# Layer 1's q projection computed transposed, for two tiles at a time

## The reference

```
x = x + tanh(g_xattn[0]) * L0_xattn(layernorm(x), ctx)   # 32 heads of 128, 8 key/value heads, rms-normed q and k
x = x + tanh(g_ffn[0])   * L0_ffn(layernorm(x))          # routed LoRA: 8 experts of rank 16
x = x + tanh(g_xattn[1]) * L1_xattn(layernorm(x), ctx)   # 16 heads of 96, 4 key/value heads, q and k not normed
x = x + tanh(g_ffn[1])   * L1_ffn(layernorm(x))          # silu(gate) * up, then down
```

```
q = (latents @ Wq.T).reshape(b, q_len, H, HD)            # H = 16, HD = 96
q = q.transpose(0, 2, 1, 3).reshape(b, KV, G, q_len, HD) # KV = 4 groups of G = 4 heads
scores = einsum('bkgqd,bksd->bkgqs', q, k) * scale       # contracted over the 96 of a head
```

## Time and profile before

| | us |
|---|---|
| median of 3 runs | 1289.04 |
| lowest and highest run | 1287.67, 1289.56 |
| the profiled execution: its own time | 1291.96 |
| the profiled execution: span from first to last instruction | 1290.1 |

### The profile page before, as it was taken

How to read it: one execution, slowest core, us unless ns; L and a number is a source line. 1 busy time by engine, 2 the same in 40 slices (tenths; PEclk the granted TensorE clock), 3 DMA queues, 4 the chain that set the end, 5 groups by cost and what they waited for, 6 DMA issues and landing times.

```text
span 1290.1 us, 24439 instructions
## 1 busy us (share of the span) xinstructions
PE 1254.1 (97%) x7392; PEld 1103.9 (86%) x7392; DVE 962.0 (75%) x2425; ACT 830.8 (64%) x2867; POOL 582.9 (45%) x1029
## 2 busy tenths in 40 slices
PE   8799999999999999999999989999999999999998
PEld 7698888888888888888888878899999999878886
DVE  7778777867787787787778888887777778963434
ACT  6677777767777777787778655576666666632221
POOL 3566555556565565566555642332333323540000
PEclk9899999999999999999999999999999999999999
DMA  6465465554455654544655431333543324370000
GB/s 211 92 131 115 83 135 105 113 110 103 102 115 103 130 106 95 123 109 86 134 113 101 102 71 34 69 72 70 103 91 66 85 57 101 73 179 1 33 1 33
DMA packets 339078, 121.11 MB, mean 94 GB/s; under 512 B 307104, under 2 KB 325280, under 8 KB 338976
## 3 DMA queue, kind: packets, MB, share of 16 engines
q1 hardware_dynamic: 313888, 84.59, 34.3%
q10 hardware_dynamic: 21104, 29.12, 7.9%
q0 software_dynamic: 3984, 6.29, 2.0%
HBM read 39.21 MB, written 2.10 MB: 32 GB/s over the span
## 4 chain that ended last, share of the span: by engine, by line
PE 52%; DVE 17%; ACT 14%; issue 5%; POOL 5%; DMA 5%; SPq 0%; ACTq 0%; DVEq 0%; POOLq 0%
PE bank L575 13%; PE bank L577 13%; PE bank L576 13%; PE bank L816 7%; DVE split L1217 5%; DMA turned<-scratch 4%; PE bank L834 4%; DVE scratch L1291 3%; ACT scratch L941 3%; POOL rq L1666 3%; ACT scratch L916 3%; ACT bank L904 3%; DVE mx L1300 2%; ACT pieces L953 2%; PE bank L670 1%
## 5 line engine op out<-in xcount | busy, mean ns | idle before, releaser
L575 PE MATMUL bank<-split 128*128 128x256 f32 (+6 forms) x2120 | 704.0, 332 | 19.5 <-DVE split L1217 8.3
L576 PE MATMUL bank<-split 128*128 128x256 f32 (+6 forms) x2120 | 692.4, 327 | 0.0
L577 PE MATMUL bank<-split 128*128 128x256 f32 (+6 forms) x2120 | 692.4, 327 | 0.0
L575 PEld LDWEIGHTS bank<-split 128*128 128x128 f32 (+2 forms) x2120 | 403.0, 190 | 67.1 <-DVE split L1217 19.1
L577 PEld LDWEIGHTS bank<-split 128*128 128x128 f32 (+2 forms) x2120 | 402.7, 190 | 34.7
L576 PEld LDWEIGHTS bank<-split 128*128 128x128 f32 (+2 forms) x2120 | 403.3, 190 | 30.8
L1647 POOL CAST split<-turned 128x512 fp32r<-128x512 f16 x384 | 234.5, 640 | 289.0 <-DMA turned<-pieces 287.8
L870 ACT ACTIVATE split<-bank 96x256 fp32r<-96x256 f32 (+6 forms) x392 | 165.2, 432 | 81.4 <-PE bank L670 43.8
L1217 DVE TENSOR_TENSOR split<-bank,split 96x256 fp32r<-96x256 f32 (+6 forms) x392 | 185.4, 475 | 26.4 <-ACT split L870 20.1
L941 ACT ACTIVATE scratch<-bank,nb,w_max 128x256 f32<-128x256 f32 x256 | 141.5, 563 | 73.0 <-DVE nb L1303 72.8
L953 ACT ACTIVATE pieces<-scratch,rs 128x256 f16<-128x256 f32 x384 | 171.7, 509 | 8.7 <-DVE rs L1315 7.3
(11 more groups left out here) (82 smaller groups left out, 1268.7 us busy)
## 6 DMA issues: line engine op xcount, KB each, us to landing
raw<-in_wq_a ACTq DMA_DIRECT2D x14, 512.0 KB, 4.2
raw<-in_wo_a ACTq DMA_DIRECT2D x14, 512.0 KB, 3.8
raw<-in_wkv_a ACTq DMA_DIRECT2D x7, 512.0 KB, 6.7
turned<-pieces SPq DMA_TRANSPOSE x192, 3.3
raw<-in_wq_c ACTq DMA_DIRECT2D x8, 384.0 KB, 3.4
craw<-in_ctx_t SPq DMA_DIRECT2D x8, 256.0 KB, 3.5
raw<-in_wo_c ACTq DMA_DIRECT2D x4, 512.0 KB, 3.8
split<-in_down_t POOLq DMA_DIRECT2D x2, 1024.0 KB, 5.8
```

The source lines that it names most:

```text
L575: pe.matmul(out, whi, mhi, start=start, stop=False)
L576: pe.matmul(out, whi, mlo, start=False, stop=False)
L577: return pe.matmul(out, wlo, mhi, start=False, stop=stop)
```

## The change

Layer 1's q is now computed with the dimensions on the partitions at once, for two tiles together: the weights (128 of their columns at a time) are the operand that is held, and the tokens of two tiles (256 columns) are streamed. There are three chunks of 128 columns of weights, each with four slices of the contraction and three matmuls, 36 of 256 columns for two tiles. Half of them (18) are done in the step of the even tile, half in that of the odd (`q_turned(..., half)`). `q_evac` and `q_turn` are gone.

A chunk holds the 96 dimensions of one of the first three heads and 32 dimensions of the fourth. For that the split of the weights writes them in another order, with two instructions for each slice in place of one (`q_block`, `qp` = 2). The result lies in bank 6 and a part of bank 3, and is moved by five copies on ACT and five subtractions on DVE for two tiles (`qT_moves`: 96 x 512, 96 x 256 and three of 32 x 256 from partitions 96 to 127), in the steps in which the second half was projected. On DVE these five stand ahead of `y_add`; before, the one stood behind it.

In the LoRA stage a first half needs the next tile's normed tokens, which are written in the same step. There (`late_q`: four steps, for the pairs of the first group that begin with tiles 0, 2, 4 and 6) it stands behind `lora_project_out`, and the turn of k (`k_turn`, `k_evac`, `k_low`) moves behind it. The low parts of layer 1's first q weights for k = 1 and 2 move from the end of step 4 of layer 0's last group into step 5, behind the low parts of the normed tokens.

```diff
+        def q_block(L, w, k):
+            block = flat(w)[:, k * L.qw:(k + 1) * L.qw]
+            if L.qp == 1:
+                return [block]
+            by_chunk = chunks(block, L.oc)
+            return [by_chunk[:, :, 0:L.hd], by_chunk[:, :, L.hd:P]]
...
+            def q_turned(L, g, b, half):
+                s = attn[L.name]
+                gb, tile = g + b // NT, b % NT
+                if half == 0:
+                    if starts(g, b):
+                        pe.wait_ge(attn[L0.name].qb_done, NH * L0.tiles)
+                    else:
+                        pe.wait_ge(s.qlo_done, two_tiles(g, b, 0))
+                    if is_at(L, g, L1, 0) and b < NT:
+                        pe.wait_ge(norm[2].lo, tile + 2)
+                for c in range(L.oc):
+                    out = bank[6][:, c * 2 * P:(c + 1) * 2 * P] if c < 2 else bank[3][:, 0:2 * P]
+                    for k in range(KC):
+                        if (c * KC + k >= L.oc * KC // 2) != bool(half):
+                            continue
+                        if tile == 0 and c == 0 and k == 3:
+                            pe.wait_ge(s.wq_lo, (gb + 1) * L.qp)
+                        if tile == 0 and c == 0 and k < 3:
+                            pe.wait_ge(s.wq_lo_rest, (gb * 3 + (k + 1)) * L.qp)
+                        at_c = k * L.qw + c * P
+                        last = mm3(out, tuple(flat(w)[:, at_c:at_c + P] for w in wq),
+                                   at(xT, slice(None), k, slice(tile * P, (tile + 2) * P)),
+                                   start=k == 0, stop=k == KC - 1)
+                if half:
+                    last.then_inc(s.q_done, 1)
...
-                    pe.wait_ge(s.qlo_done, count(g, b, 1, 1))
+                    pe.wait_ge(s.qlo_done, two_tiles(g, b, 1))
...
                 values(L, g, b, second)
                 if lora is not None:
                     lora_project_out(lora)
+                if late:
+                    q_turned(*three, 0)
+                if late and two[0] is L1:
+                    k_turn(*two)
                 if prev is not None:
                     project(*prev, beside_norm)
-                if three is not None and three[0] is L1:
-                    q_turn(*three)
...
             def qt_evac(L, g, b):
                 s = attn[L.name]
-                act.wait_ge(s.qt_done, count(g, b, 1, 1))
-                copy(flat(qT[b % 2][0])[0:L.hd, :], bank[6][0:L.hd, :]).then_inc(s.qthi_done, 1)
+                act.wait_ge(s.q_done, g * (NT // 2) + (b // 2 + 1))
+                for rows, heads, src in qT_moves(L):
+                    copy(qT_two[rows, 0, heads], src).then_inc(s.qthi_done, 1)
...
                     norm_low(*beside_norm)
+                if scaled:
+                    q_lo(L1, 0, 1)
+                    q_lo(L1, 0, 2)
...
                     norm_stats(2, lora)
+                if three is not None and three[0] is L1 and three[2] % 2:
+                    qt_low(*two)
                 if prev is not None:
                     y_add(*prev)
...
-                if three is not None and three[0] is L1:
-                    qt_low(*three)
-                if new_q is not None:
+                if new_q is not None and not ahead:
                     q_lo(*new_q, 1)
```

More of the change, by code:

```diff
@@ L204, in beside, with late_q @@
     return norm, lora, second
+def late_q(L, g, b):
+    three = later(L, g, b, 3)
+    return beside(L, g, b)[2] is not None and three is not None and three[0] is L1 and three[2] % 2 == 0
 def scales_ahead(L, g, b):
@@ L1065, in step @@
                 else:
-                    if three is not None:
-                        q_evac(*three)
-                    if three is not None and two is not None and two[0] is L1:
+                    late = late_q(L, g, b)
+                    if three is not None and two is not None and two[0] is L1 and not late:
                         k_evac(*two)
@@ L1071, in step @@
                         probs_high(*one, 1)
+                    if two is not None and two[0] is L1 and late:
+                        k_evac(*two)
                 if beside_norm is not None and beside_norm[0] > 1:
@@ L1439, in step @@
                     probs_low(*one, 0)
[L1440 removed]
+                late = late_q(L, g, b)
+                if three is not None and kv is not None and kv[0] is L1 and not late:
                     k_low(*kv)
@@ L1443, in step @@
                     probs_low(*one, 1)
+                if kv is not None and kv[0] is L1 and late:
+                    k_low(*kv)
                 if new_o:
```

103 lines of the change are left out of this document (53 added, 50 removed).

## The result

The changed kernel took 1317.27 us (median of four runs, 1312.91 to 1321.47), the kernel before beside it 1289.30 (1287.67 to 1292.99): ratio 1.0213, interval 1.0166 to 1.0259. It is 28 us slower. 12 were forecast (1301.4), and the range ended at 1311.

The account below looks back on a forecast made before the run. PE was taken to set the pace, with PE and DVE waiting in turn in the LoRA stage. -9.0 + 4.5 + 5.0 + 10.2 + 1.7 = +12.4 gave 1301.4 us from the median 1289.04; range 1288 to 1311.

Parts of the forecast that it names:

- PE's own work and the scores' wait: Outside the LoRA stage: PE saves 0.36 in each of 25 steps (-9.0); scores wait 0.35 in 13 steps (+4.5).
- The stage: LoRA stage: +10.2 (5 to 13), mainly q and k's turn behind the values in four late steps; 11.9 with its clock.
- the rival: LoRA stage: the clock falls in every late step, 5.1 more than the forecast, 1306.5; chance 0.20.
- The other terms, 10.2: LoRA stage without the clock: late steps +7.8, three steps between save 1.1, DVE's work not covered by its pauses +3.5.
- The weights' new wait: Changes of group in layer 1: PE waits 1.65 for the third weight slice at each of three, +5.0 (0.9 to 2.4 each).
- The clock: Late steps of the LoRA stage: one fall to half clock after a new wait, +1.7, from 0 to 4 x 1.7.
- DVE falls behind for good: Rival: lows at their high ends, weights 2.4 and scores 0.65 each, +18.6 in all, 1307.6; chance 0.10.

Follow-up runs that it names:

- the first experiment: Changed kernel with idle turns of the identity on PE in the four late steps, 16 ahead of the LoRA turn, 6 ahead of the values: 1311.17 us, ratio 1.0162.

## Why the prediction was wrong

*PE's own work and the scores' wait*: right. 0.36 a step less, 0.35 of wait in each second step; 20.18 for two steps is 0.39 less than before, forecast 0.37. The 0.35 was taken from between 0 and 0.65, so its hitting is in part luck. The five copies that I counted without overlap lay in 2.07 (2.1 forecast): one of the four places between them overlaps, by 0.12.

*The stage*: +13.1 against 11.9. The mechanism was in the main the one described: in the late steps PE has nothing to put into the wait, and q comes behind the values. (Most of the wait in the step shown, 1.74 of 2.41, is for the LoRA activations and not for the tile's low part.) The late halves cost some 12 us with the clock. But the clock fell in all four of them, as the rival had it, and not in one: 9.2 us of half clock, of which some 5.4 came back with the turns of the identity, where I had 1.7. The other terms, 10.2, were then too large by 2 to 3. That the stage's sum came out so near is luck.

*The weights' new wait*, "1.65 at each of three changes of group": the step that failed. The three changes cost 13.8 where 3.9 were forecast. The wait was 2.52, beyond its high end of 2.4. The 1.67 for q's lows was about right (2.39 for 0.68: 1.71). The first two slices took 1.77 for 0.55 and 0.87, 0.35 more where I had 0.2; the third took 1.35 for 0.71, 0.64 more where I had 0.1. With these the same sum gives 1.71 + 0.35 + 0.64 + 0.32 - 0.64 = 2.38. The rule of the Trainium skill that I had set against it (SBUF — State Buffer, Who interferes with whom) says that such an instruction and one of GpSimd exclude each other from a port; the trace agrees, since the piece beside GpSimd's subtraction (960.86 for 0.98) took 1.18 and one of the same form ahead of it 0.45, and by that sentence the wait was to be nearer 2.4. But the longer wait is only 0.9 in each of three changes, 2.6 of the 9.9 that were missing. The larger part is what the sum had at nothing: the wait was priced by itself. What it brings with it, the fall of the clock (the row from 875; 6.5 us of half clock at the three changes, of which 4.9 came back with the turns) and DVE's work that is still behind when the next step begins, made 4.2, 4.2 and 5.5 of it.

*The clock*, "one fall, 1.7": eight stretches at half clock in the changed kernel's trace, three in that before. I had no row for a wait shorter than 3.87 in the stage. In the changed kernel waits of 0.35 to 2.18, mostly two or three close together, went with seven falls (the eighth lies behind one of 3.09); but with the lows behind the residual 2.13 to 2.18 at each change went with none. And a fall does not cost all of its half clock: 17 us of it, taken away, gave 7 to 10, because PE is not always what the step waits for.

*The last group*: not in the sum at all. I had judged DVE's room from 900 to 940 (29.7 of 40). From 1080 to 1120 it was 35.0 of 40 already in the kernel before (its row stands above), which the same view would have told me. Two tiles' lows in one step of that group gave +4.7.

So the rival *DVE falls behind for good* was near, with its place wrong: it does so for a step or two at a time, wherever another load falls on the same step, and it catches up between. I had let the average of a stretch decide it. The forecast was short by 14.6 (27.0 against 12.4): the changes 9.9, the last group 5.1, the stage 1.2, less 1.6 elsewhere (of which 1.1 lies behind the last values).

## What to carry to other kernels

Work that is joined for two tiles comes every second step as a double load. Ask of each engine that carries it whether it has room in the fullest step in which it falls (a change of weights, a stage with a second job, an epilogue), not on the average: here 1.5 us of DVE's time for each of 16 pairs was worth 14 us. Ask too whether joining makes more work: three pieces of 32 rows cost here what three of 96 do. And a new wait on TensorE is priced with the clock that may fall behind it, and with what the late engine still owes to the next step; idle turns of the identity in a free bank show what that part is, before anything else is rebuilt.

## What the runs showed of the hardware

- Waits of nearly one length were followed by a fall of the clock once and not another time: in the kernel before 2.66 us at 61.4 (0.57 in the row from 65), in the changed kernel 2.62 at the same place of the program and none:

```profile
64.00:69.00 5.00, 5.00 (x42) 4.91 (x41) 3.74 (x8) 2.53 (x10) 4.75 (x9) 1.00 0.66 120
```

- At the changes of group waits of 0.35 and 2.17 were followed by a fall three times in three in the changed kernel; with the lows behind the residual a wait of 2.13 to 2.18 was followed by none in three.
- A piece of DVE's weights (128x288, two operands in SBUF) took 0.45 us alone and 1.18 beside GpSimd's subtraction. Four pieces beside GpSimd's took 2.25 us; six of which only the last lay wholly beside it took 2.33.
- DVE's subtraction of 32x256 took 0.427 us, that of 96x256 0.411: fewer rows made it no shorter.
- Turns of the identity kept the clock at 1.00 through waits of 2 to 4 us (the 36 turns in the long wait of the kernel before, the row from 754.5); in the first experiment, where a wait of 3.08, or two of 1.08 and 0.78, were left in the same step, it fell there all the same.
